# A mixture-of-experts tail: where the low parts of the dense units are made, and how early the sort stands

## What is computed

```
x = x + conv1x1(softmax(f(x)^T g(x)) h(x))          # conv attention, 32 channels
t = tokens(x)
t = t + LN(t) + causal_attention(LN(t))              # softmax over the query axis
for e in range(8):                                   # top 2 of 8 experts
    h = silu(LN(t) @ W1[e]) @ W2[e]                  # 128 -> 512 -> 128
    t += combine[:, e:e+1] * h
```

## Time and profile before

| | |
|---|---|
| median of 3 runs | 145.19 us (144.94 to 145.34) |
| the profiled execution | 145.2 us, its span 143.4 us |
| mean granted clock of TensorE | 0.952 of full speed |
| busy: PE, DVE, ACT, POOL | 119.4, 99.2, 91.0, 72.3 us of the span |
| dense units, first to last | about 45 to 99 us from the span's start |
| sorted blocks | about 102 to 140 us |

### The profile page before, as it was taken

One profiled execution on the slowest core, in us unless ns is written; L12 is line 12 of the kernel. 1 busy time (PEld: TensorE's weight loads), 2 busy tenths in 40 slices (PEclk: granted clock), 3 DMA queues, 4 the chain that ended last, 5 costly groups with the idle time before them and its releaser, 6 DMA issues.

```text
span 143.4 us, 2914 instructions
## 1 busy us (share of the span) xinstructions
PE 119.4 (83%) x870; PEld 74.7 (52%) x870; DVE 99.2 (69%) x289; ACT 91.0 (63%) x204; POOL 72.3 (50%) x100
## 2 busy tenths in 40 slices
PE   5499699999977699989999825994399699999961
PEld 1395487778754243354554302341368477777730
DVE  0555749875999799369999980196448877877660
ACT  3346964767868989989897730574056357656721
POOL 6538698489396663333733198888003331233300
PEclk9999959999999999999999995599869999999999
DMA  2349999400000006920000001100920200000002
GB/s 82 83 104 333 339 332 304 107 0 5 0 0 0 0 5 238 278 77 0 0 0 0 5 19 38 38 26 33 219 64 5 73 0 7 0 5 0 0 5 73
DMA packets 12838, 10.38 MB, mean 72 GB/s; under 512 B 1196, under 2 KB 10640, under 8 KB 12824
## 3 DMA queue, kind: packets, MB, share of 16 engines
q1 hardware_dynamic: 12424, 9.64, 23.3%
q0 software_dynamic: 352, 0.54, 1.2%
q10 hardware_dynamic: 48, 0.02, 0.0%
HBM read 8.10 MB, written 2.10 MB: 71 GB/s over the span
## 4 chain that ended last, share of the span: by engine, by line
PE 46%; DVE 15%; issue 14%; ACT 10%; POOL 7%; DMA 6%; POOLq 0%; ACTq 0%; DVEq 0%
PE bank L1557 4%; POOL rows_dram L631 3%; PE bank L1545 3%; PE bank L1569 2%; ACT hid L838 2%; PE bank L1442 2%; PE bank L1305 2%; PE bank L1547 2%; PE bank L1546 2%; PE bank L1571 2%; PE bank L1401 2%; POOL hidl L619 2%; DMA rows_dram<-rows,slot_at 2%; DMA xT<-in_x_dram 2%; ACT hidh L836 2%
## 5 line engine op out<-in xcount | busy, mean ns | idle before, releaser
L836 ACT ACTIVATE hidh<-bank 128x512 f16<-128x512 f32 x32 | 19.5, 609 | 12.6 <-PE bank L1625 12.4
L619 POOL TENSOR_TENSOR hidl<-hid,hidh 128x512 f16<-128x512 f32 x16 | 19.1, 1199 | 16.2 <-ACT hid L838 16.0
L642 POOL TENSOR_TENSOR hidl<-hid,hidh 128x512 f16<-128x512 f32 x7 | 8.2, 1179 | 27.1 <-ACT hid L800 27.1
L798 ACT ACTIVATE hidh<-bank 128x512 f16<-128x512 f32 x15 | 9.0, 597 | 17.6 <-PE bank L1547 17.5
L1252 DVE TENSOR_TENSOR hidl<-hid,hidh 128x512 f16<-128x512 f32 x16 | 14.7, 917 | 7.1 <-ACT hid L838 7.0
L838 ACT ACTIVATE hid<-bank 128x512 f32<-128x512 f32 x32 | 19.4, 608 | 0.0
L1606 PE MATMUL bank<-hidl,W2hl 128*128 128x512 f16 x32 | 12.9, 403 | 5.6 <-POOL hidl L619 5.1
L1623 PE MATMUL bank<-zh,W1h 128*128 128x512 f16 x32 | 12.7, 396 | 1.4 <-ACT hid L838 1.3
L631 POOL DMA_INDIRECT rows_dram<-rows,slot_at x8 | 10.4, 1305 | 5.5 <-issue 5.5
L1603 PE MATMUL bank<-hidh,W2hl 128*128 128x512 f16 x32 | 12.9, 403 | 0.0
L1604 PE MATMUL bank<-hidh,W2hl 128*128 128x512 f16 x32 | 12.7, 398 | 0.0
(11 more groups left out here) (256 smaller groups left out, 345.5 us busy)
## 6 DMA issues: line engine op xcount, KB each, us to landing
W1f<-in_L_ffn_W_dram SPq DMA_DIRECT2D x8, 256.0 KB, 5.4
W2f<-in_L_ffn_W_dram SPq DMA_DIRECT2D x8, 256.0 KB, 5.7
gates<-gates_dram SPq DMA_DIRECT2D x8, 256.0 KB, 5.4
rows_dram<-zero_row SPq DMA_DIRECT2D x1, 990.0 KB, 10.4
xg<-rows_dram SPq DMA_DIRECT2D x5, 198.0 KB, 4.1
xT<-in_x_dram SPq DMA_DIRECT2D x2, 256.0 KB, 2.7
out_dram<-acc SPq DMA_DIRECT2D x1, 256.0 KB, 2.1
out_dram<-total SPq DMA_DIRECT2D x2, 128.0 KB, 1.8
```

The lines of the kernel that those rows point to most:

```text
L619: pool.tensor_tensor(hidl[:, c, :], hid[:, c, :], hidh[:, c, :], ALU.subtract).then_inc(low_pool, 1)
L836: act.activation(hidh[:, c, :], pUP[c % 2][:, :], ACT.Silu, scale=1.0 / (XS * WS)).then_inc(high_ready, 1)
```

## The change

From the fifth expert on, VectorE makes the low parts of all four chunks, and GpSimd those of chunks 0 and 2 for experts 0 to 3 only: 8 and 24. GpSimd's order after unit 15 holds the four scatter steps and nothing else. On VectorE chosen stands right behind top_two_half, and first_slots, slots, gate_slots and blocks between units 14 and 15; on TensorE places stands between units 15 and 16. weights_low:5 now follows unit 16, weights_low:6 unit 19. identh is made on GpSimd in slot_constants. The blocks behind the dense units keep their split.

```diff
--- before.py
+++ after.py
@@ -84,7 +84,7 @@
     LAG = 3
     HB = 4
     POOL_WEIGHTS = 2
-    POOL_LOW = ((0, 2),)
+    POOL_LOW = tuple((e, c) for e in range(4) for c in (0, 2))
 
 
 
@@ -97,8 +97,8 @@
         normT:2 values:1 logits:1 normT:3 keys:2 values:2 read:0 logits:2 keys:3 read:1
         values:3 logits:3 finalT:0 read:2 finalT:1 read:3 route:0 unit:0 unit:1 unit:2
         finalT:2 unit:3 gatesT:0 unit:4 unit:5 unit:6 unit:7 unit:8 finalT:3 unit:9 unit:10
-        unit:11 route_half:0 unit:12 unit:13 unit:14 unit:15 unit:16 unit:17 residual:0
-        unit:18 unit:19 places:0 unit:20 unit:21 unit:22 unit:23 unit:24 unit:25 unit:26 unit:27 unit:28
+        unit:11 route_half:0 unit:12 unit:13 unit:14 unit:15 places:0 unit:16 unit:17 residual:0
+        unit:18 unit:19 unit:20 unit:21 unit:22 unit:23 unit:24 unit:25 unit:26 unit:27 unit:28
         unit:29 unit:30 unit:31 turn:0 turn:1"""
     SCALAR_ORDER = """
         tokens_high:0 tokens_high:1 relus:0 relus:1 relus:2 tokens_copy:0 relus:3 exp0:0
@@ -122,9 +122,9 @@
         norm1:1 rec1:3 scale_values:3 add1:2 tokens_low:0 stats1:2 tokens_low:1 aggr1:2
         route_copy:0 add1:3 top_two:0 norm1:2 unit:0 unit:1 one_hots:0 gate_tokens:0 unit:2
         stats1:3 aggr1:3 weights_low:2 unit:3 norm1:3 unit:4 unit:5
-        weights_low:3 unit:6 unit:7 unit:8 unit:9 rows_low:2 unit:10 unit:11 top_two_half:0
-        unit:12 weights_low:4 rows_low:3 unit:13 unit:14 chosen:0 unit:15 gate_slots:0 unit:16
-        weights_low:5 unit:17 weights_low:6 unit:18 unit:19 first_slots:0 slots:0 unit:20 blocks:0
+        weights_low:3 unit:6 unit:7 unit:8 unit:9 rows_low:2 unit:10 unit:11 top_two_half:0 chosen:0
+        unit:12 weights_low:4 rows_low:3 unit:13 unit:14 first_slots:0 slots:0 gate_slots:0 blocks:0 unit:15
+        unit:16 weights_low:5 unit:17 unit:18 unit:19 weights_low:6 unit:20
         unit:21 unit:22 weights_low:7 unit:23 unit:24 unit:25 unit:26 unit:27 unit:28
         unit:29 unit:30 unit:31 turn_copy:0 turn_copy:1 slot_gates:0"""
     GPSIMD_ORDER = """
@@ -132,9 +132,7 @@
         rstd0:0 rstd0:1 residual:0 residual:1 rstd0:2 rstd0:3 weights_scale:1
         first_weights_low:0 rstd1:0 rstd1:1 residual:2 residual:3 first_weights_low:1
         rstd1:2 unit:0 unit:1 unit:2 rstd1:3 unit:3 unit:4 unit:5 unit:6 unit:7 unit:8
-        unit:9 unit:10 unit:11 unit:12 unit:13 unit:14 unit:15 unit:16 unit:17 unit:18
-        unit:19 unit:20 scatter:0 unit:21 unit:22 scatter:1 unit:23 unit:24 scatter:2 unit:25 unit:26
-        scatter:3 unit:27 unit:28 unit:29 unit:30 unit:31"""
+        unit:9 unit:10 unit:11 unit:12 unit:13 unit:14 unit:15 scatter:0 scatter:1 scatter:2 scatter:3"""
     WARM_UP = 4
 
     def in_order(order):
@@ -460,12 +458,11 @@
 
         block = ctx.enter_context(nc.Block())
 
-        def low_part(h, e, c):
-
-            by_pool = c in POOL_LOW[h]
-            per = [len(chunks) if by_pool else FC - len(chunks) for chunks in POOL_LOW]
-            return (low_pool if by_pool else low_dve,
-                    h * E * per[0] + e * per[h] + sum((q in POOL_LOW[h]) == by_pool for q in range(c + 1)))
+        def low_part(e, c):
+
+            by_pool = (e, c) in POOL_LOW
+            done = sum(((u // FC, u % FC) in POOL_LOW) == by_pool for u in range(e * FC + c + 1))
+            return low_pool if by_pool else low_dve, done
 
         def unit_before(h, e, c, back):
 
@@ -482,7 +479,7 @@
 
         def low_block(n):
 
-            return (low_pool, UNITS // 2 + n // 2 + 1) if n % 2 else (low_dve, UNITS // 2 + n // 2 + 1)
+            return (low_pool, len(POOL_LOW) + n // 2 + 1) if n % 2 else (low_dve, UNITS - len(POOL_LOW) + n // 2 + 1)
 
         BN_IN = 16 * 7
         BN_G_IN = 16 * 3
@@ -567,6 +564,7 @@
                 pool.memset(all_ones[:, :], 1.0).then_inc(slots_set, 1)
                 pool.memset(earlier[:, :], 1.0).then_inc(zero_set, 1)
                 pool.memset(before[:, :, :], 1.0).then_inc(zero_set, 1)
+                pool.memset(identh[:, :], 0.0).then_inc(zero_set, 1)
                 pool.iota(token_row[:, :], pattern=[[1, HN]], base=1, channel_multiplier=0,
                           allow_small_or_imprecise_dtypes=True).then_inc(slots_set, 1)
                 pool.iota(block_at[:, :], pattern=[[P, NBR]], base=0, channel_multiplier=0,
@@ -575,7 +573,9 @@
                           allow_small_or_imprecise_dtypes=True).then_inc(slots_set, 1)
                 pool.iota(row_meta[:, :, 0:1], pattern=[[P, HT], [1, 1]], base=1, channel_multiplier=1,
                           allow_small_or_imprecise_dtypes=True).then_inc(token_set, 1)
-                pool.wait_ge(zero_set, 5)
+                pool.wait_ge(zero_set, 6)
+                pool.affine_select(out=identh[:, :], in_=identh[:, :], compare_op=ALU.not_equal, fill=1.0,
+                                   base=0, pattern=[[-1, P]], channel_multiplier=1).then_inc(identh_ready, 1)
                 pool.affine_select(out=earlier[:, :], in_=earlier[:, :], compare_op=ALU.is_ge, fill=0.0,
                                    base=-1, pattern=[[1, P]], channel_multiplier=-1).then_inc(slots_set, 1)
                 pool.affine_select(out=before[:, :, :], in_=before[:, :, :], compare_op=ALU.is_ge, fill=0.0,
@@ -610,7 +610,7 @@
                 rstd(b, mv1, ve1, rstd1, mv1_ready, ve1_ready, rstd1_ready)
 
             def unit(h, e, c, parity):
-                if c not in POOL_LOW[h]:
+                if (e, c) not in POOL_LOW:
                     return
                 n = (h * E + e) * FC + c
                 pool.wait_ge(hid_ready, n + 1)
@@ -1104,7 +1104,6 @@
 
             def chosen_experts(_):
 
-                dve.tensor_copy(identh[:, :], ident[:, :]).then_inc(identh_ready, 1)
                 dve.wait_ge(topi_ready, 2 * HT)
                 index = topi[:, HT:2 * HT, 0:2].rearrange("p t k -> p k t").unsqueeze(3).broadcast_to([P, 2, HT, E])
                 lane = iota_e[:, :].unsqueeze(1).unsqueeze(1).broadcast_to([P, 2, HT, E])
@@ -1602,7 +1601,7 @@
                 pe.wait_ge(high_ready, (h * E + e) * FC + c + 1)
                 pe.matmul(o, W2hl[:, e, c, 0, :], hidh[:, c, :], start=(c == 0), stop=False)
                 pe.matmul(o, W2hl[:, e, c, 1, :], hidh[:, c, :], start=False, stop=False)
-                pe.wait_ge(*low_part(h, e, c))
+                pe.wait_ge(*low_part(e, c))
                 pe.matmul(o, W2hl[:, e, c, 0, :], hidl[:, c, :], start=False,
                           stop=(c == FC - 1)).then_inc(down_done, 1)
```

## The result

Six runs of the changed kernel gave a median of 143.44 us (142.44 to 143.96), six of the kernel before on the same chip 145.26 (144.55 to 145.76): ratio 0.9878, 95% interval 0.9838 to 0.9918. It is faster by 1.2%; 6.3% was forecast, and the stated range ended 1.9 us lower, at 141.5. The profiled execution took 143.42 us around a span of 141.7.

What follows compares the result with a forecast made beforehand. GpSimd's eight scatters and low parts, delaying each other in one queue, were taken to set the end. First turn 102.16 to 92.95 saves 9.2, identity costs 0.1: 145.2 - 9.2 + 0.1 = 136.1 us, range 132.0 to 141.5.

Steps and rivals of the forecast that it cites:

- rival B: Scatters locked out almost always, entering only at VectorE gates or gaps; first turn 98.3, 141.4 us; 14%.
- (c): GpSimd's scatters under busy VectorE: five at 2.4 us, two at 1.56; last at 87.3, first turn 92.95.
- (b): Eight low parts move from GpSimd to VectorE; smallest slack some 0.4 us, TensorE's dense half ends at 90.7, not 99.28.
- (a): Sort moved up on VectorE and TensorE: first scatter at 72.2 instead of 81.94, nothing lost at unit 15's low part.
- the prediction's 81.3: Start of the last scatter if, by the skill's inference on descriptor generation, no scatter were held.
- (d): Identity made on GpSimd by memset and affine_select: costs 0.1 us, between 0 and 0.5.
- (e): Behind the first turn the sorted blocks keep their old course: 41.24 us to the end of the span.
- A: No scatter is held; rows arrive before the dense half ends, third turn's copy gains about 1.8: 133.4 us; 24%.
- C: Scatters hold VectorE, 7.7 us in all, so TensorE waits for its low parts: 140.7 us, half of it 137; 8%.
- D: Not even gates or short gaps admit scatters; all eight wait for VectorE's last add at 92.4: 150.0 us, slower; 3%.

Runs made afterwards that it cites:

- e6: Changed kernel plus twelve waits of VectorE for its own last result between its operations, units 15 to 25: 138.06 us, ratio 0.9512 to the kernel before.
- e8: Changed kernel plus seven reductions of a 128x256 tile, one SBUF input each, among VectorE's operations: 138.80 us, ratio 0.9570 to the kernel before.
- e3: Changed kernel with the eight indirect writes replaced by plain writes of the same size, rows not placed by slot: 136.35 us, ratio 0.9411 to the kernel before.
- e12: Changed kernel's split of low parts, sort at its old place, plus five self-waits of VectorE: 139.41 us, ratio 0.9606 to the kernel before.
- e1: Changed kernel with identh copied on VectorE again, now behind unit 29: 143.25 us, ratio 0.9883 to the kernel before.
- e9: Changed kernel plus seven self-waits of VectorE, with the first two turns, their copies and slot_gates ahead of unit 31: 135.67 us, ratio 0.9379 to the kernel before.
- e7: Changed kernel plus seven reductions of a 128x32 tile, one SBUF input each, among VectorE's operations: 142.35 us, ratio 0.9815 to the kernel before.
- e2: Changed kernel plus twelve one-column memsets among VectorE's operations, units 15 to 25: 143.91 us, ratio 0.9915 to the kernel before.
- e10: Changed kernel run again with no instruction changed, as a control: 143.59 us, ratio 0.9889 to the kernel before.

## Why the prediction was wrong

The direction was right and the mechanism of the loss stood there as rival B, at 14%. From the forecast's 136.1 to 143.4 are 7.3 us, all of it ahead of the first turn, which came 7.6 late (100.51 against 92.95): the first scatter 2.8 late, the eight scatters 5.5 longer, and the delivery from the last scatter to the turn 0.7 shorter (4.97 against the 5.63 carried over; why it was shorter is open).

**(c), the scatters under a busy VectorE, is the step that failed.** From the first to the last scatter's start it had 15.1 us; it was 20.6 (95.54-74.96), 5.5 more. Its "between 1.15 and 3.03" took the 3.03 us row as the dear end. It wasn't one: that scatter was let go because VectorE fell idle at 85.56, as the prediction itself noted, so 3.03 was a wait cut short, a lower bound. The three cheap rows, 1.15, 1.25 and 1.12, were no sample of a busy VectorE either; two of them met a gate or a gap. The price was to be read from VectorE's own order: the time to the next gate, plus about 1 us. Gates stand 4.8 us apart (78.52, 83.33, 88.14), which gives 4.65, 4.34 and 4.49. B had that rule, with three scatters at gates, and its 141.4 fell short by the late start. The runs confirm the rule from both sides: openings give scatters of 1.0 to 1.7 us (e6, e8), plain writes are not held (e3). That it is the read of the indices, and not another part of the indirect form (more descriptors to write, say), is inferred from e3 alone and not shown.

(c) also let VectorE run out of work too early, at 84.8; it ran without a gap until 90.61. By (b)'s own figures low 23 was to end at 83.0. Unit 23 starts at 78.8 there, and a low part begins 1.97 us behind its unit's start, so low 23 could have ended at 81.4: VectorE was 1.6 us behind. At 1.58 us gained per expert (3.6 in 5.18) it catches up near 88, and with the 2.8 us of (a) near 90.7.

The rule has an exception, and the row of 1.25 us, which the prediction put down to a gate or a gap, is one. That scatter ended at 96.22 in the kernel before. VectorE's low part from 93.26 ran to 95.36 and the addition behind it to 95.97, both with two SBUF inputs:

```profile
95.29 0.68 DVE L1244 TENSOR_TENSOR acc<-acc,gated 128x512 f32<-128x512 f32 x1
96.13 0.69 DVE L1252 TENSOR_TENSOR hidl<-hid,hidh 128x512 f16<-128x512 f32 x1 [0.16 <-ACT hid L838]
```

It ended 0.93 us after the addition began, as others end 0.9 to 1.1 after a gate begins. In e12 the same happens behind a self-wait, on GpSimd's and VectorE's timelines:

```profile
82.79 1.45 POOL L631 DMA_INDIRECT rows_dram<-rows,slot_at  x1 [0.30 <-issue]
```

```profile
82.70 0.68 DVE L1236 SCALAR_TENSOR_TENSOR W1l<-W1f,W1h 128x512 f16<-128x512 f32 x1
83.30 0.68 DVE L1239 SCALAR_TENSOR_TENSOR W2hl<-W2f,W2hl 128x512 f16<-128x512 f32 x1
```

The records of VectorE differ between the two cases. Over all kept traces, scatters were kept out across 98 starts of a two-input operation right behind another operation; these 98 operations lasted 0.670 to 0.676 us. Where one got in at such a start with no gate or reduction just before it, the operation lasted 0.678 or more. So a gap, or a GpSimd low part that holds VectorE up (as before the 1.25), seems to open VectorE's next starts too, not only itself. What changes in VectorE there is open, and no run tests it.

The Trainium skill (SBUF — State Buffer, section Who interferes with whom) says that a VectorE instruction with two SBUF inputs contends with a GpSimd instruction that reads SBUF. The rows of 4.3 to 4.7 us agree, for indirect scatters. Its inference that descriptor generation isn't held by such instructions agrees with e3's 0.55 us, but doesn't cover an indirect transfer; the prediction's 81.3 for it doesn't come out of its own terms either (72.2+7x1.26 is 81.0). The section's sentence "Issue order, not op shape, decides who blocks" doesn't match the scatter from 74.96, which stood until the gate at 78.52 while five two-input operations began behind it (75.51 to 77.91).

**(a) put the first scatter at 72.2; it came at 74.96, 2.8 late.** The steps behind the first slot step were right: 2.88 us, as forecast. That step came at 72.08, not 69.36. Of this 1.4 is the clock of the first 30 us: e3, with the same code and no fall, has the step at 70.68. The other 1.3 are meetings I had priced at nothing: chosen took 0.78 us, about 0.4 of it for its comparison beside a GpSimd low part, where the wait it was to fall into was 0.54, and VectorE's low 13 took 1.65 beside GpSimd's of unit 14 (69.58), 1.0 too long. The work moved up lands where GpSimd still makes low parts.

**(b) held.** TensorE waited for no GpSimd low part; for VectorE it waited once, 0.66 us, where 0.4 of slack was worked out. The dense half ended at 93.16, not 90.7; 1.4 of this is the early clock and 0.66 that wait. It ceased to be the bound, though, so of the 6.1 us that it gained only 1.65 reached the first turn.

**(d)** was priced at 0.1 and reached TensorE as 0.4 (e1 against the changed kernel), too little to show in the time. **(e) held to 0.1:** 141.7-100.51 = 41.2 us against 41.24.

Against the rivals: A needed a free port; e3 shows what that gives, 136.35 and not 133.4. The first block stood at 94.03 instead of 93.0, behind VectorE's tail, and from there to the end of the span are 40.7 us instead of A's 38.6, with a granted clock of 0.50 from 95 to 98 us. e9 took 39.2 from its first block, at a clock of 1.00 there. C is false: no VectorE operation was held beside the eight scatters. The row it rested on isn't repeated either: the low part at 92.37 starts 0.61 into a scatter, as that at 93.26 had 0.60 into its own, and takes 0.69 where that took 2.10. D's condition, that a gate doesn't admit a scatter, didn't occur.

## What to carry over

Where VectorE runs operations with two SBUF inputs back to back, price an indirect DMA on GpSimd by the time to VectorE's next gap or one-input operation of the size of a gate, plus 1 us, read from VectorE's order (a 128x32 one is not to be counted on); filling VectorE's last gaps with more work makes this worse. A stall that ended because the other engine fell idle is a lower bound for the price, not its upper end. If the transfer is on the path, a self-wait of 0.11 us on VectorE ahead of each is the cheapest opening found here; whether fewer would do wasn't tried. And compare the early part of a kernel over several profiles: here a clock fall between 16 and 30 us moved what follows by up to 1.5 us.

## What was not expected

- A scatter that needs 0.96 us alone was shut out by six VectorE operations in a row, one under way when it began and five begun behind it, and this three times running: 4.65, 4.34, 4.49. VectorE lost nothing by it.
- A two-input 128x512 operation of VectorE lasts 0.67 us (at most 0.676) where it keeps a scatter out and 0.68 where one gets in at its start without a gate or reduction before it.
- 0.04 us between two records admit it (e6), while a 128x32 reduction, 0.09 us of VectorE's time, often doesn't (e7). A memset isn't an opening at all (e2).
- The same code lost its clock at 26 us in one profile and at 16 to 23 us in another (e10); code that is the same up to there kept it (e3). Why is open.
